# First stage of a two-layer graph network: the last removal round of each block without its ranks and its removal, with the order of the steps planned anew

## The chip, the cores and the metric

The kernel runs on one core of one Trainium2 chip, as one launch. The metric is the device time of that launch in microseconds (us); lower is better. Engine names are those of the profile: PE is TensorE (PEld its weight loads), DVE is VectorE, ACT is ScalarE, POOL is GpSimd, SP is SyncE, which here issues nearly all transfers.

## What is computed

The inputs are node features `x` (16 graphs, 1024 nodes, 128 features), a weighted adjacency `adj` (16 x 1024 x 1024, some 6% of it nonzero, diagonal set) and a node mask. Two layers follow, and the change touches only the stage that holds the first one.

```python
# layer 0
h = maximum(layernorm(x), 0)
for W, b in three layers:
    h = h @ W + b
    nh = h / maximum(norm(h), 1e-12)
    h = (adj * (nh @ nh.T)) @ h          # relu but for the last
x = x + h
# layer 1
keep = dilate(adj > 0)                   # below
h = three SAGE convolutions with batch norm on adj * keep, and a last linear map
x = x + h
```

`dilate` goes through the nodes of a graph in order. For node n it counts the neighbours that are left (num), takes sf = ceil(num/2) if num > 10 and 1 otherwise, ranks the neighbours by a running count, and removes those whose rank is a multiple of sf, from row n and from column n at once. So earlier rows change the later ones. This removal depends on `adj` alone and not on layer 0.

## The kernel before, in words

**Stages.** `build` runs four stages one behind the other: a short setup, `layer0` (the first stage of this text), `layer1_middle` and `layer1_last`. Between the first two a branch looks at one flag; if it is above zero, `dilate_all` computes the removal anew the slow way. With these inputs it is not taken.

**Two jobs in one stage.** `layer0` does layer 0 and the removal side by side.

Layer 0 is 48 *units* (16 graphs x 3 layers, lines 42 and 316 to 403), two graphs interleaved. A unit has a head and a body. The head: the product with W (`ha`, PE, L683), bias (`hb`, DVE, L869), squares with their sums (`sq`, ACT, L784), the norm (`hc`, `hd`, L873, L789, L877), the rows scaled by 1/norm (`hd`, ACT, 8 instructions at L794), 8 transposes (`hf`, PE, L639), and two copies to PSUM's outside, a rounded part (`hf`, ACT, L801) and the rest (`ho`, DVE, L881). For the first layer of a graph a layer norm comes ahead of it: statistics (`lna`, DVE, L852 and L855), 8 scaled copies (`lnb`, ACT, L767), 8 transposes (`lnc`, PE, L639). The body is 16 steps (8 blocks of 128 rows x 2 halves of 512 columns), done in pairs: two cosine tiles of three matmuls each (L702 to L704), two products with the adjacency on DVE (`cos`, L889), two aggregations (`agg`, L711, two records each). A cosine tile waits until DVE has read the tile two before it (one PSUM bank for each half). The head of unit u+1 is worked in among the body of unit u.

The removal is 32 *blocks*: 4 quads of graphs x 8 blocks of 128 rows. A block does four graphs at once. Within a block the rows depend on each other, so the kernel iterates: it guesses which entries of the diagonal 128 x 128 part go, counts, and corrects the guess, ROUNDS = [2, 3, 4, 6, 6, 3, 3, 8] times for the eight blocks of a quad, 35 rounds a quad and 140 in all. A round is
- `rank` on PE (L734, 4 matmuls into PSUM bank D0): running counts;
- `rule` on DVE (L953 to L967, 9 instructions on 4 columns): sf and the constants of each row;
- `rank` on ACT (L822, 4 instructions): the ranks of the entries, read from D0;
- `drop` on DVE (L974, 1 instruction): what remains, written to one of two tiles `Sd`.

After the last round come `bias` (DVE, L981 to L992), `check` (DVE, L1000: the last two guesses must agree, else the flag counts up) and the 8 `wide` steps, which carry the result to all 1024 columns: PE (L744, 4 matmuls into the one bank D1), ACT (L832, 2 instructions), DVE (L1006). The next block of the same quad needs the wide steps (`low` on DVE, L905 and L909) and then starts with `cross` (DVE, L921 and L925, which also reuses `check`'s scratch tile `Au`) and `base`. Rows of the adjacency come in by SP (L615) and become signs on ACT (`row`, L815), then a transpose by DMA (`fill`, L600). Finished tiles are transposed back (`flip`, L608) and multiplied (`mask`, DVE, L1018); each of these 256 mask tiles is stored by SP (L621) from a ring of three. Two quads run interleaved, first 0 and 1, then 2 and 3.

**What sets the order.** Every engine gets its instructions as one list, and the lists are made at build time by a planner (`Planner.order`, L245). Each step has a cost in ns, a rank (lower goes first) and what it comes after:

```python
def add(self, engine, name, cost, rank, after=(), chain=None, takes=None, frees=None):
...
rank = s.rank - (t - ready) / AGING
if best is None or (t, ENGINES.index(e), rank, ready) < best[:4]:
```

The planner plays the stage through with these costs and writes down the order in which the steps start; `takes` and `frees` stand for rings of buffers and the two PSUM banks. On the chip the order of each engine is fixed by this list, and only semaphores move the times. If a cost is too short in the plan, the engine that waits for the step is given it too early and stands still. SP's issue of a transfer has a cost of 70 in the plan (L242).

The steps that this text comes back to, with their plan costs: `lnb` 1610 (L339, L390), `hd` on ACT 1610 (L350), `row` 620 (L423), `check` 610 at rank 6 (L441), `mask` 620 at rank 3 (L454), `rank` on ACT 1365 (L438), `drop` 610 (L439).

## Time and profile before

| | |
|---|---|
| median of 3 runs | 2694.39 us (2693.61 to 2701.42) |
| the profiled execution | 2693.11 us, its span 2691.3 us |
| PE busy, whole span | 2579.7 us, 96% |
| DVE busy | 2076.1 us, 77% |
| ACT busy | 1459.3 us, 54% |
| first aggregation of layer 0 to its last | 34.7 to 1625.3 us |
| mean granted TensorE clock | 0.993 of full speed |

The span is the time between the first and the last instruction of the program; 1.8 us of the profiled execution lie around it. The first stage is the first 1626 us. Busy times are unions of the instructions' durations. Matmuls are pipelined, and a record's duration reaches over the start of the next.

### The profile page before, as it was taken

The numbers are of one execution on the slowest core, as the hardware profiler recorded it, in microseconds if no ns is written. First come the engines' busy times: TensorE is split into PE (matmuls) and PEld (weight loads), VectorE is DVE, ScalarE is ACT, GpSimd is POOL, SyncE is SP. The second block draws the span as 40 slices with busy tenths as digits, with TensorE's granted clock in tenths as the row PEclk, the third lists the DMA queues.
The fourth block names the chain that finished last, engine by engine and source line by source line (L and its number), as shares of the span: only waits on it lengthen the run. The fifth ranks groups of instructions, "written<-read, shape, count | busy, mean of one in ns | idle before, by whom it ended". The sixth has DMA issues, their size and how long they took to land. (4 is left out here: it accounts for less than half of the span.)

```text
span 2691.3 us, 38914 instructions
## 1 busy us (share of the span) xinstructions
PE 2579.7 (96%) x12390; PEld 1630.3 (61%) x12390; DVE 2076.1 (77%) x5328; ACT 1459.3 (54%) x4324; POOL 562.7 (21%) x233
## 2 busy tenths in 40 slices
PE   6999999999999999899999998999999999999898
PEld 4666656656655666566666654555555555555897
DVE  4778889888988888888988877766666636776676
ACT  5667747766655776567656321322322344443676
POOL 0000000000000000000000002766666603433673
PEclk9999999999999999999999999999999999999999
DMA  7354275265367244536433323555555419996663
GB/s 235 89 148 147 57 187 156 65 160 167 77 170 220 83 136 133 128 100 192 114 112 120 83 69 140 195 191 192 193 192 192 182 55 384 404 402 263 249 233 153
DMA packets 325878, 455.48 MB, mean 169 GB/s; under 512 B 155680, under 2 KB 218528, under 8 KB 325664
## 3 DMA queue, kind: packets, MB, share of 16 engines
q1 hardware_dynamic: 325664, 452.89, 51.9%
q8 instruction: 102, 1.67, 0.3%
q14 instruction: 112, 0.92, 0.1%
HBM read 352.13 MB, written 67.11 MB: 156 GB/s over the span
## 5 line engine op out<-in xcount | busy, mean ns | idle before, releaser
L711 PE MATMUL a_acc<-a_ew,a_Hr 128*128 128x512 f32 x1536 | 751.9, 600 | 0.5 <-ACT a_hT L807 0.4
L889 DVE TENSOR_TENSOR a_ew<-adj,a_cos 128x512 f32<-128x512 f32 x768 | 508.6, 682 | 68.3 <-PE a_cos L704 66.0
L1720 POOL TENSOR_TENSOR b_dsum<-adj 128x1024 f32<-128x1024 f32 x15 | 133.3, 8885 | 1797.4 <-DVE adj L1628 1797.4
L702 PE MATMUL a_cos<-a_nh 128*128 128x512 f32 x768 | 413.3, 538 | 14.0 <-DVE a_ew L889 7.3
L711 PEld LDWEIGHTS a_acc<-a_ew,a_Hr 128*128 128x128 f32 x1536 | 275.2, 190 | 160.7 <-issue 112.2
L832 ACT ACTIVATE a_v<-a_D,a_wb,a_small 128x256 f16<-128x256 f32 x512 | 287.8, 635 | 86.4 <-PE a_D L744 84.5
L704 PE MATMUL a_cos<-a_nh,a_nl 128*128 128x512 f32 x768 | 304.1, 396 | 0.0
L703 PE MATMUL a_cos<-a_nl,a_nh 128*128 128x512 f32 x768 | 301.6, 393 | 0.0
L822 ACT ACTIVATE a_vr<-a_D,a_small 128x128 f16<-128x128 f32 x560 | 209.4, 456 | 135.3 <-DVE a_small L967 134.7
L1383 PE MATMUL b_acc<-adj,b_z 128*128 128x512 f32 x512 | 225.0, 592 | 0.0
L1480 PE MATMUL b_acc<-adj,b_z 128*128 128x512 f32 x512 | 222.5, 592 | 0.0
L815 ACT ACTIVATE a_Ab<-stage 128x512 fp8e4<-128x512 f32 x256 | 156.7, 633 | 111.2 <-DMA stage<-in_adj 110.5
L1724 POOL TENSOR_TENSOR b_dsum<-b_dsum,adj 128x1024 f32<-128x1024 f32 x90 | 211.4, 2349 | 12.9
L702 PEld LDWEIGHTS a_cos<-a_nh 128*128 128x128 f32 x768 | 145.5, 189 | 101.4 <-issue 44.1
L1018 DVE TENSOR_TENSOR a_kp<-a_T,stage 128x512 fp8e4<-128x512 fp8e4 x256 | 170.0, 686 | 41.4 <-DMA scr_keep<-a_kp 39.2
L1006 DVE SCALAR_TENSOR_TENSOR a_T<-a_v,a_Ab 128x512 fp8e4<-128x512 f16 x256 | 172.2, 685 | 29.0 <-ACT a_v L832 28.6
L703 PEld LDWEIGHTS a_cos<-a_nl,a_nh 128*128 128x128 f32 x768 | 146.3, 191 | 64.2 <-issue 51.4
L1480 PEld LDWEIGHTS b_acc<-adj,b_z 128*128 128x128 f32 x512 | 96.0, 190 | 114.3 <-issue 113.1
L704 PEld LDWEIGHTS a_cos<-a_nh,a_nl 128*128 128x128 f32 x768 | 144.7, 188 | 33.4
L1383 PEld LDWEIGHTS b_acc<-adj,b_z 128*128 128x128 f32 x512 | 94.8, 190 | 107.1 <-issue 107.1
L784 ACT ACTIVATE h<-a_Hr 128x128 f32<-128x128 f32 x384 | 113.1, 299 | 69.2 <-DVE a_Hr L869 69.1
L1515 ACT ACTIVATE b_z<-b_o 128x128 f32<-128x128 f32 x256 | 75.3, 297 | 116.9 <-DVE b_o L1699 100.6
(269 smaller groups left out, 4337.6 us busy)
## 6 DMA issues: line engine op xcount, KB each, us to landing
adj<-in_adjT SPq DMA_DIRECT2D x108, 1024.0 KB, 12.8
adj<-in_adjT SPq DMA_DIRECT2D x128, 512.0 KB, 4.3
stage<-in_adj SPq DMA_DIRECT2D x256, 256.0 KB, 3.3
scr_keep<-a_kp SPq DMA_DIRECT2D x256, 64.0 KB, 1.8
scr_z<-b_zT SPq DMA_DIRECT2D x32, 512.0 KB, 3.6
scr_ag<-b_a SPq DMA_DIRECT2D x32, 512.0 KB, 3.3
stage<-scr_keep SPq DMA_DIRECT2D x13, 1024.0 KB, 7.5
b_kp<-scr_keep SPq DMA_DIRECT2D x12, 1024.0 KB, 7.8
```

Source lines behind the costliest of these rows:

```text
L702: e.matmul(cos[j][:], n[:, blk(k)], n[:, half(j)], start=True, stop=False)
L703: e.matmul(cos[j][:], n[:, blk(k)], m[:, half(j)], start=False, stop=False)
L704: e.matmul(cos[j][:], m[:, blk(k)], n[:, half(j)], start=False, stop=True).then_inc(E["cos"], 1)
L711: e.matmul(acc[j][:], Hr[u % 2][:, k, :], ew[idx % EW][:], start=(k == 0), stop=(k == NK - 1)).then_inc(E["agg"], 1)
L822: e.activation(vr[p][:, i, :], D0[:, i, :], ACT.Abs, bias=sm[p]["b2"][:, i:i + 1], scale=sm[p]["sc"][:, i:i + 1]).then_inc(T["vr"], 1)
L832: t = e.activation(v[c % 3][:, g * 256:g * 256 + 256].rearrange("p (x s) -> p s x", s=2), D1[:, 2 * g:2 * g + 2, :], ACT.Abs, bias=wb[p][: ...
L889: e.tensor_tensor(ew[idx % EW][:], adj[g % 2][:, k, half(j)], cos[j][:], ALU.mult).then_inc(E["ew"], 1)
L1006: e.scalar_tensor_tensor(TT[:, slot, 2 * j:2 * j + 2, k].rearrange("p m x s -> p m (x s)"), v[c % 3][:].rearrange("p (m c) -> p m c", m=2) ...
L1018: e.tensor_tensor(as_blocks(kp[c % 3][:]), row_half(slot, j, q), turned[:, :, :, :, q % 2], ALU.mult, saturate=False).then_inc(T["kp"], 1)
L1383: t = e.matmul(acc[j][:], src[:, q, :], adj[n % 3][:, q, half(j)], start=(q == 0), stop=(q == NK - 1))
L1480: t = e.matmul(acc[j][:], z[m % 2][:, q, :], adj[slot(m)][:, q, half(j)], start=(q == 0), stop=(q == NK - 1))
L1724: e.tensor_tensor(d, d, b[:, q, :], ALU.add).then_inc(E["ds"], 1)
```

## The change

1. In the last round of a block, `rank` on ACT (4 instructions) and `drop` on DVE (1 instruction) are gone. `rank` on PE and `rule` stay, since the wide step needs the constants; D0 is free when `rule` is done.
2. The 8 `wide` steps on PE read the guess of the round before, and so may start a round earlier. Their ACT part waits for `bias` as before.
3. `check` waits for the wide steps that contain the block's own diagonal part, computes from them and `X` what `drop` would have, with one DVE instruction more, waits for that, and compares as before.
4. Costs and ranks of the plan are other numbers, so that the lists of all engines come out anew: `lnb` 3080, `hd` 2340, `sq` at rank 0, `row` 540, `mask` 605 at rank 2, `check` 1220. The arithmetic of these steps is as before, and the layer norm's scaled copies are ACT's as before.
5. One semaphore more. The form of `frees` is another, with the same meaning for the flips.

```diff
@@ -19,7 +19,7 @@
 NK = 8
-BANK = 76
+BANK = 77
 MAGIC = 8388608.0
@@ -30,7 +30,7 @@
 MID = 1
-SQ = 1
+SQ = 0
 GAP = 0.2
@@ -291,7 +291,7 @@
             if s.frees:
-                ring, key = (s.frees, s.name) if s.frees in rings else (s.frees[0], s.frees)
+                ring, key = (s.frees, s.name) if s.frees in rings else s.frees
                 free[ring][held[(ring,) + key]] = s.end
@@ -336,7 +336,7 @@
             add("dve", ("lnb", g), 400, 1, [("act", "lna", g)])
-            add("act", ("lnb", g), 1610, 0, [("dve", "lnb", g)] + ([("pe", "hf", 0)] if g == 1 else []))
+            add("act", ("lnb", g), 3080, 0, [("dve", "lnb", g)] + ([("pe", "hf", 0)] if g == 1 else []))
             add("pe", ("lnc", g), 880, 0, [("act", "lnb", g)] + bank)
@@ -347,7 +347,7 @@
         add("dve", ("hd", v), 210, 1, [("act", "hc", v)])
-        add("act", ("hd", v), 1610, 0, [("dve", "hd", v)])
+        add("act", ("hd", v), 2340, 0, [("dve", "hd", v)])
         add("pe", ("hf", v), 880, 0, [("act", "hd", v)])
@@ -420,7 +420,7 @@
                          None, "af")
-                add("act", ("row", n, i, j), 620, 2, [("dma", "row", n, i, j)], None, None, "af")
+                add("act", ("row", n, i, j), 540, 2, [("dma", "row", n, i, j)], None, None, "af")
             transfer(("fill", n, i), 800, freed + [("act", "row", n, i, j) for j in range(2)])
@@ -434,14 +434,16 @@
             add("pe", ("rank", n, r), 260, 1, [("dve", "drop", n, r - 1)] if r else ready, None, "D0")
-            add("dve", ("rule", n, r), 1140, 3, [("pe", "rank", n, r)] + ([] if r else [("dve", "base", n)] + done))
-            add("act", ("rank", n, r), 1365, 1, [("dve", "rule", n, r)], None, None, "D0")
-            add("dve", ("drop", n, r), 610, 3, [("act", "rank", n, r)] + ([] if r else [("dve", "cross", n)]))
+            add("dve", ("rule", n, r), 1140, 3, [("pe", "rank", n, r)] + ([] if r else [("dve", "base", n)] + done), None,
+                None, ("D0", ("rank", n, r)) if r == K - 1 else None)
+            if r < K - 1:
+                add("act", ("rank", n, r), 1365, 1, [("dve", "rule", n, r)], None, None, "D0")
+                add("dve", ("drop", n, r), 610, 3, [("act", "rank", n, r)] + ([] if r else [("dve", "cross", n)]))
         add("dve", ("bias", n), 700, 3, [("dve", "rule", n, K - 1)])
-        add("dve", ("check", n), 610, 6, [("dve", "drop", n, K - 1)])
+        add("dve", ("check", n), 1220, 6, [("dve", "wide", n, i, k // 4) for i in range(Q)])
         for i in range(Q):
             for j in range(2):
-                add("pe", ("wide", n, i, j), 330, 1, [("dve", "drop", n, K - 1)], None, "D1")
+                add("pe", ("wide", n, i, j), 330, 1, [("dve", "drop", n, K - 2)], None, "D1")
                 add("act", ("wide", n, i, j), 960, 1, [("pe", "wide", n, i, j), ("dve", "bias", n)], None, "v", "D1")
@@ -450,8 +452,8 @@
                     for q in (2 * m, 2 * m + 1):
-                        last = ("flip", quad, i, m, j) if q % 2 else None
-                        add("dve", ("mask", quad, i, q, j), 620, 3, [("dma", "flip", quad, i, m, j),
+                        last = ("flip", ("flip", quad, i, m, j)) if q % 2 else None
+                        add("dve", ("mask", quad, i, q, j), 605, 2, [("dma", "flip", quad, i, m, j),
                             ("dve", "wide", quad * NK + q, i, j)], f"flip{quad}{i}{m}{j}", "kp", last)
@@ -476,7 +478,7 @@
                    "bst bag lnsd lnrs lnm lnr " + " ".join(f"adj{i}{k}" for i in range(2) for k in range(NK)))
-        T = P.sems("at0 at1 fl0 fl1 fl2 fl3 af0 af1 af2 sign low au x bs b0 b1 ct ru vr sd v8 wb wd av rw kp kps0 kps1 kps2 sum tot flag")
+        T = P.sems("at0 at1 fl0 fl1 fl2 fl3 af0 af1 af2 sign low au x bs b0 b1 ct ru vr sd again v8 wb wd av rw kp kps0 kps1 kps2 sum tot flag")
         W, rows = P.sb("W", [128, 3, 128]), P.sb("rows", [128, 3, 128])
@@ -650,6 +652,8 @@
                         e.wait_ge(T["b0"], nth["dve", "base", a[0]])
+                    elif kind == "rank" and a[1] == ROUNDS[a[0] % NK] - 1:
+                        e.wait_ge(T["ru"], 9 * nth["dve", "rule", a[0], a[1]])
                     elif kind == "rank":
@@ -737,12 +741,12 @@
                     k, K, p = n % NK, ROUNDS[n % NK], n // NK % 2
-                    e.wait_ge(T["sd"], nth["dve", "drop", n, K - 1])
+                    e.wait_ge(T["sd"], nth["dve", "drop", n, K - 2])
                     take("D1", step)
 ...
                         t = e.matmul(D1[:, b:b + 2 - odd, :],
-                                     Sd[p][K % 2][:, i, :] if q == k else at_blocks(Q * p + i, q, k),
+                                     Sd[p][(K - 1) % 2][:, i, :] if q == k else at_blocks(Q * p + i, q, k),
                                      C["UL"][:, 0:128 if odd else 256], start=(b == 0), stop=(b == 3),
@@ -992,8 +996,12 @@
                     n, = a
-                    p, c = n // NK % 2, nth["dve", "check", n]
-                    e.wait_ge(T["sd"], nth["dve", "drop", n, ROUNDS[n % NK] - 1])
+                    k, p, c = n % NK, n // NK % 2, nth["dve", "check", n]
+                    e.wait_ge(T["rw"], max(nth["dve", "wide", n, i, k // 4] for i in range(Q)))
+                    e.wait_ge(T["ct"], nth["pe", "rank", n, ROUNDS[k] - 1])
+                    e.scalar_tensor_tensor(Sd[p][ROUNDS[k] % 2][:], TT[:, slots(n), k // 2, k, :, k % 2], 0.0, X[p][:],
+                                           ALU.is_equal, ALU.is_lt, saturate=False).then_inc(T["again"], 1)
+                    e.wait_ge(T["again"], c)
                     e.wait_ge(T["x"], earlier("dve", "cross", step))
```

In the diff the hunk at line 387 is left out; it sets the same cost of `lnb` (1610 to 3080) for the last graph. A line of three dots stands for unchanged lines.

## Rows read from the trace of the kernel before

**Rows 1.** Page: span, busy time by engine, and the 40 slices.
```profile
span 2691.3 us, 38914 instructions
PE 2579.7 (96%) x12390; PEld 1630.3 (61%) x12390; DVE 2076.1 (77%) x5328; ACT 1459.3 (54%) x4324; POOL 562.7 (21%) x233
...
DVE  4778889888988888888988877766666636776676
ACT  5667747766655776567656321322322344443676
```
**Rows 2.** Windows: stretch, length, busy of PE, PEld, DVE, ACT, POOL, clock, DMA.
```profile
0.00:1626.00 1626.00, 1547.40 (x7722) 985.57 (x7722) 1366.09 (x3689) 1017.84 (x2843) 1.54 (x9) 1.00 0.47 131
1626.00:2691.30 1065.30, 1032.28 (x4668) 644.75 (x4668) 710.05 (x1639) 441.44 (x1482) 561.19 (x224) 0.99 0.61 228
...
200.00:400.00 200.00, 191.42 (x965) 121.91 (x965) 171.74 (x495) 133.93 (x374) 0.00 (x0) 0.98 0.49 129
1200.00:1400.00 200.00, 196.28 (x1023) 125.26 (x1021) 178.56 (x452) 140.53 (x383) 0.00 (x0) 1.00 0.50 142
```
**Rows 3.** Windows of single units, columns as above.
```profile
362.50:397.30 34.80, 31.64 (x147) 19.49 (x145) 29.53 (x65) 14.56 (x44) 0.00 (x0) 0.95 0.90 218
1078.60:1115.10 36.50, 31.60 (x141) 19.84 (x141) 29.34 (x48) 22.25 (x58) 0.00 (x0) 1.00 0.64 155
911.30:943.70 32.40, 32.40 (x180) 20.86 (x177) 25.00 (x58) 26.59 (x69) 0.00 (x0) 1.00 0.47 130
1510.10:1538.80 28.70, 27.70 (x106) 17.52 (x105) 24.34 (x40) 7.33 (x28) 0.00 (x0) 1.00 0.36 85
```
**Rows 4.** Waits of PE, 100 to 1500 us: total us, times, longest.
```profile
PE a_pp L639 <- ACT h L767: 13.1, 14, 1.7
PE a_D L744 <- ACT a_v L832: 11.4, 8, 3.6
PE a_pp L639 <- ACT h L794: 7.9, 11, 3.2
PE a_cos L702 <- DVE a_ew L889: 6.0, 7, 1.3
PE a_cos L702 <- DVE a_nl L881: 3.3, 7, 1.0
```
**Rows 5.** Waits of DVE, 100 to 1500 us.
```profile
DVE a_ew L889 <- PE a_cos L704: 40.7, 58, 1.5
DVE a_kp L1018 <- DMA scr_keep<-a_kp: 27.8, 31, 2.4
DVE a_T L1006 <- ACT a_v L832: 25.7, 34, 3.4
DVE a_Sd L974 <- ACT a_vr L822: 25.0, 33, 2.0
```
**Rows 6.** Groups by line in the first stage: busy, mean ns of one.
```profile
L832 ACT ACTIVATE a_v<-a_D,a_wb,a_small 128x256 f16<-128x256 f32 x512 | 287.8, 635 | 86.4 <-PE a_D L744 84.5 <-DVE a_T L1006 1.8
L822 ACT ACTIVATE a_vr<-a_D,a_small 128x128 f16<-128x128 f32 x560 | 209.4, 456 | 135.3 <-DVE a_small L967 134.7
L1018 DVE TENSOR_TENSOR a_kp<-a_T,stage 128x512 fp8e4<-128x512 fp8e4 x256 | 170.0, 686 | 41.4 <-DMA scr_keep<-a_kp 39.2
L974 DVE SCALAR_TENSOR_TENSOR a_Sd<-a_vr,a_X 128x512 fp8e4<-128x512 f16 x140 | 96.1, 686 | 27.0 <-ACT a_vr L822 26.8
L925 DVE SCALAR_TENSOR_TENSOR a_X<-a_T,a_Au 128x512 fp8e4<-128x512 fp8e4 x32 | 22.1, 692 | 1.1
L1000 DVE SCALAR_TENSOR_TENSOR a_Au<-a_Sd 128x512 fp8e4<-128x512 fp8e4 x32 | 22.0, 687 | 0.4
```
**Rows 7.** Timeline of ACT, end of block 3: start, us.
```profile
309.37 2.45 ACT L794 ACTIVATE h<-a_Hr,a_rnrn 128x128 f32<-128x128 f32 x8 [0.77 <-DVE a_rnrn L877]
311.73 1.48 ACT L822 ACTIVATE a_vr<-a_D,a_small 128x128 f16<-128x128 f32 x4
313.10 1.01 ACT L801 ACTIVATE a_nh<-a_pp 128x1024 fp32r<-128x1024 f32 x1
```
**Rows 8.** Line L767, eight scaled copies of a layer norm: ns min/median/max.
```profile
L767 ACT ACTIVATE h<-h,a_lnnm,a_lnrs x120: 477/479/497, 8.7 to 1458.4; 128x128 f32<-128x128 f32 x120
```
**Rows 9.** Timeline of DVE, three places.
```profile
53.49 0.69 DVE L921 SCALAR_TENSOR_TENSOR a_Au<-a_Ab,tri 128x512 fp8e4<-128x512 fp8e4 x1 [0.91 <-DMA a_T<-a_Ab]
54.22 0.69 DVE L925 SCALAR_TENSOR_TENSOR a_X<-a_T,a_Au 128x512 fp8e4<-128x512 fp8e4 x1
54.83 0.68 DVE L889 TENSOR_TENSOR a_ew<-adj,a_cos 128x512 f32<-128x512 f32 x1
...
312.46 0.18 DVE L992 TENSOR_TENSOR a_wb<-a_wb,a_small 128x16 f32<-128x16 f32 x1
313.24 0.69 DVE L974 SCALAR_TENSOR_TENSOR a_Sd<-a_vr,a_X 128x512 fp8e4<-128x512 f16 x1 [0.59 <-ACT a_vr L822]
313.96 0.69 DVE L1000 SCALAR_TENSOR_TENSOR a_Au<-a_Sd 128x512 fp8e4<-128x512 fp8e4 x1
...
1089.23 0.68 DVE L889 TENSOR_TENSOR a_ew<-adj,a_cos 128x512 f32<-128x512 f32 x1
1093.36 0.69 DVE L1006 SCALAR_TENSOR_TENSOR a_T<-a_v,a_Ab 128x512 fp8e4<-128x512 f16 x1 [3.45 <-ACT a_v L832]
```
**Rows 10.** Timeline of ACT at the longest stall of PE.
```profile
1085.39 1.12 ACT L832 ACTIVATE a_v<-a_D,a_wb,a_small 128x256 f16<-128x256 f32 x2 [0.34 <-PE a_D L744]
1091.69 0.63 ACT L815 ACTIVATE a_Ab<-stage 128x512 fp8e4<-128x512 f32 x1 [5.17 <-DMA stage<-in_adj]
1092.23 1.10 ACT L832 ACTIVATE a_v<-a_D,a_wb,a_small 128x256 f16<-128x256 f32 x2
```
**Rows 11.** Masks on DVE and aggregations on PE: first and last start.
```profile
L1018 DVE TENSOR_TENSOR a_kp<-a_T,stage x256: 641/685/695, 329.3 to 1583.9; 128x512 fp8e4<-128x512 fp8e4 x128
...
L711 PE MATMUL a_acc<-a_ew,a_Hr x1536: 590/592/1061, 34.7 to 1625.3; 128*128 128x512 f32 x192
```

More of the change, by code:

```diff
@@ L389, in plan_units @@
     add("dve", ("lnb", G), 400, 1, [("act", "lna", G)])
-    add("act", ("lnb", G), 1610, 1, [("dve", "lnb", G), ("pe", "hf", 3 * G - 1)])
+    add("act", ("lnb", G), 3080, 1, [("dve", "lnb", G), ("pe", "hf", 3 * G - 1)])
     add("act", ("first", 0), 920, 3, [("act", "lnb", G)])
```

## The prediction

> **What bounds the kernel now.** I read the page first. The program has 38914 instructions in 2691.3 us; PE is busy 96% of it, DVE 77%, ACT 54% [rows 1]. The DVE slices stand at 8 and 9 from the fourth to the 21st and are lower behind it: the removal loads DVE in the first stage. The windows then split the span: the first stage is 1626 us with 1547 us of PE, 1366 of DVE and 1018 of ACT; the other 1065 us hold nothing that the change touches, so they stay as they are [rows 2]. In the middle of the stage both engines are nearly full at once: from 200 to 400 us PE 191 and DVE 172 of 200, from 1200 to 1400 us PE 196 and DVE 179 [rows 2]. The clock stood at 0.98 to 1.00 of full speed there, its upper level of 2.4 GHz.
>
> Then I cut out single units of layer 0. A unit in which the removal makes no rounds any more takes 28.7 us. One with rounds but no masks takes 32.4 us; two with rounds and masks take 34.8 and 36.5 us, though PE had 31.6 us of busy time in both [rows 3]. So the stage's time is the sum of PE's own work and of short stalls, and the stalls are worst where removal rounds, masks and bodies share DVE. The removal itself sets no end: its last mask starts at 1583.9 us and the last aggregation at 1625.3 [rows 11]. An earlier end of the removal is thus worth nothing by itself. What counts is how long PE stands.
>
> Where it stands, by PE's waits from 100 to 1500 us: 13.1 us before the transposes of a layer norm (14 times, so 0.94 each), 7.9 before those of a head (11 times, 0.72 each), 11.4 for ACT to empty D1 (8 times), 6.0 for DVE's product and 3.3 for its last copy of a head [rows 4]. That is some 42 us that can be seen. Waits of DVE in the same stretch: 27.8 for stores of masks, 25.7 and 25.0 for ACT's parts of wide step and round [rows 5].
>
> **The change, part by part.**
>
> *The last round's ranks on ACT.* 560 instructions for 140 rounds are 4 each and 209.4 us, 1.50 us a round [rows 6]. One round in each of 32 blocks goes: 32 x 1.50 = 48 us off ACT's 1018. ACT is at 63% of the stage and not the bound, so this comes through only where PE waits for ACT. In the timeline a last round's ranks (1.48 us at 311.73) stand between the end of the scaling of a head (309.37 + 2.45) and the copy at 313.10 that the head still needs [rows 7]. Of the 11.4 us for D1 the longest, 3.6, has another cause: ACT sat 5.17 us before a row of the adjacency came in, with the wide step behind it in its queue [rows 10]. I give this part 2 us, between 0 and 8 (11.4 less 3.6).
>
> *The last `drop` and the new test.* One instruction of 686 ns goes, 32 times. One of the same kind comes in `check`: 128 x 512 elements, read strided out of `a_T`, as `cross` does in 692 ns [rows 6]. So 0 us of DVE work, where I had looked for a saving. What does go is DVE's wait for ACT in that round: 25.0 us in 140 rounds, 32/140 of it 5.7 us, and at the last round of block 3 it was 0.59 us [rows 5, 9]. What comes is a wait of DVE for itself, between the test and the comparison. `cross` has the same pair: its second starts 0.73 us after the first, the next free instruction 0.61 after that one [rows 9]. So 0.12 us x 32 = 4 us more of DVE. Net 2 us of DVE given back, of which PE sees perhaps all: 2 us, between -4 and +6. The Trainium skill (VectorE: DVE Perf Modes, "The DRAIN you can't avoid") says that a semaphore between two Vector instructions costs nothing extra, since the next one waits for the pipe in any case. By it the 4 us would be 0 and the gain of this part 6; the rows speak against it, so the sum goes by them.
>
> *The wide steps' PE part a round earlier.* The same 8 x 4 matmuls. They hide beside `rank` and `rule`, but the first holds D1 until `bias` is done, and `base` of the other quad also needs D1. The trace has no such hold to read. The nearest rows bound it from both sides: if one wide step in a block finds D1 taken, or is spared a wait, that is at most one of the 11.4/8 = 1.4 us waits, and with some of 32 blocks hit either way a few us. I take 0, as the plan knows D1's ring, between -3 and +3.
>
> *`check` behind the wide steps, `cross` behind `check`.* `check` is last in rank, and the next block's `cross` needs its scratch tile. So between a block's wide steps and the next block's first `drop` stand two more instructions of 0.69 and a read-out. Against this each block's chain loses 1.50 of ACT and 0.69 of DVE and their signals, 2.2 us or more. The chain gets shorter on balance, and it has no end to set [rows 11]: 0.
>
> *New costs in the plan.* This is the largest term. Eight instructions of `lnb` at 479 ns with some 0.09 of overlap are about 3.2 us, where the old plan had 1.61; eight of `hd` took 2.45 us against 1.61 [rows 7, 8]. The old plan thus handed PE the transposes 1.5 and 0.7 us (3.08 less 1.61, 2.34 less 1.61) too early, and the stalls before them, 0.94 and 0.72 each, are of that size [rows 4]. With 3.08 and 2.34 PE is given a pair of cosine tiles or an aggregation in that time instead, and the head still has most of a 32 us unit to finish. Of 13.1 + 7.9 = 21.0 us, two thirds should go: 14 us, between 5 and 21. `row` at 540 and `check` at 1220 are small repairs. `mask` goes to rank 2, ahead of `rule` and `drop`; that is the part I trust least (below).
>
> *A new order as such.* Each unit's stalls depend on what happens to stand beside what: single units range from 28.7 to 36.5 us [rows 3]. The two with rounds and masks differ by 1.7 us; with 48 units and about 1.5 us of such scatter in each, the sum scatters by the root of 48 times that, about 10 us. I take 0 for it and keep 10 either way for the range.
>
> *Sum.* 2 + 2 + 0 + 0 + 14 = 18 us. The profiled execution took 2693.1 us (2691.3 of span and 1.8 around it), so it would take 2675; the median of the runs is 1.3 above the profiled one, which gives 2676.5.
>
> **The rivals.**
>
> *DVE is the bound, nothing comes of it (22%).* In the middle of the stage DVE was busy 172 to 179 us of 200, its work does not shrink, and and PE's stalls before cosine tiles would just grow by what those before transposes lose. Against it: in units without masks DVE had 7.4 of 32.4 us to spare [rows 3]. The Trainium skill speaks for it (Trainium Kernel Development and Optimization, "Performance Expectations"): matmul busy time is a bad measure of nearness to the limit, weight loads are the good one, and for other engines occupancy is fine. In rows: weight loads 61% in the stage, DVE 84% [rows 2]. In that case only the 2 us of DVE come out: 2692.
>
> *Masks crowd DVE (10%, slower).* At rank 2 the masks of a flip go ahead of rules and drops, in runs. They are stored from a ring of three, so the fourth in a run waits for a store, and while DVE stands there no product is made and PE stands before its next cosine tile. DVE lost 39.2 us to this in the stage [rows 6], and a unit with masks cost 2.4 to 4.1 us more than one without [rows 3]. If that wait doubled and PE saw it all, it would be +39 against the -18: 2715. It decides from about 18 us more, from which on the kernel is no faster; above 26 it is slower. For it: of SP's transfers each store stands in one queue with the rows and transposes, and these aren't repriced. Against it: 256 masks are the same number, a plan that knows the ring spreads them, and a unit of 28.7 us late in the stage, while masks still run, shows that masks alone do no harm [rows 3, 11].
>
> *Larger than forecast (8%).* If the stalls of crowded units shrink too, because rounds of 140 are 108 for ACT, and half of the 42 seen and half of the 27.8 for stores go, it is 35 us: 2659; with the hidden part of stalls, which lie inside long matmul records, 2650.
>
> *The change does not do what it says (under 1%).* The round on PE and `rule` stay, and only ACT's instructions go; that is visible in the counts and no doubt about time. I leave it in the rest.
>
> **How the numbers follow.** The forecast's case has 60%, 2660 to 2690. The range takes in the bounds of the terms: at best 8 + 6 + 3 + 21 = 38 us, so 2656, rounded to 2655; at worst the DVE rival with scatter, 2702. Beyond lie most of the masks' case and the lowest end of the larger one. A difference of 0.3%, 8 us, is about what a measurement of this kernel can tell from no change: faster means under 2686.3, slower over 2702.5. Faster: four fifths of the 60 and all of the 8, and a sixth of the rival of DVE by scatter, 0.63 in all rounded up to 0.65; slower 0.11; the same 0.24.
>
> **What would show it.** Right: L822 x432 for 560 and L974 x108 for 140, beside `check`'s two instructions of 32 each; ACT's busy time down by 48 us, DVE's within 5; PE's waits before L639 down to a third of 21 us; the second stage 1065 us as before; last aggregation near 1607; the last mask before 1584. Wrong: the waits before L639 gone and those of L702 or the mean of L702 (a stall hides in its record) grown by as much, which is the DVE rival; the DVE wait for stores well above 39 us, which is the masks'; or waits before L639 as they were, which would say that the plan's costs were not their cause.

## The result, and the profile after

The changed kernel took 2705.11 us (median of 6 runs, 2703.74 to 2706.85) against 2694.72 for the kernel before on the same chip; the ratio is 1.0033, with a 95% interval of 1.0022 to 1.0043. It is slower, by 10 us in the medians and 9 by the ratio, where I had forecast 18 us less. The profiled execution has a span of 2702.0 us.

The page of the changed kernel, its first lines:

```profile
span 2702.0 us, 38818 instructions
PE 2582.3 (96%) x12390; PEld 1642.4 (61%) x12390; DVE 2079.9 (77%) x5328; ACT 1418.1 (52%) x4196; POOL 562.3 (21%) x233
```

128 instructions of ACT are gone and its busy time fell by 41 us [rows 1], where I had put 48. DVE has the same count and 4 us more. Windows of the changed kernel, columns as in [rows 2], the stage now ending at 1636 us:

```profile
0.00:1636.00 1636.00, 1547.98 (x7722) 995.80 (x7722) 1370.01 (x3689) 977.41 (x2714) 1.55 (x9) 0.99 0.47 130
1636.00:2702.00 1066.00, 1034.29 (x4669) 646.64 (x4668) 709.92 (x1639) 440.71 (x1482) 560.74 (x224) 0.98 0.61 228
```

The second part is as long as before (1066 against 1065 us); the whole difference lies in the first stage, where PE has the same 7722 instructions and as much busy time, in 10 us more. Groups of the first stage by line, which answer to [rows 6]:

```profile
L836 ACT ACTIVATE a_v<-a_D,a_wb,a_small 128x256 f16<-128x256 f32 x512 | 287.2, 631 | 116.4 <-PE a_D L748 71.9 <-issue 31.2 <-DVE a_wb L996 10.1
L1026 DVE TENSOR_TENSOR a_kp<-a_T,stage 128x512 fp8e4<-128x512 fp8e4 x256 | 170.5, 686 | 49.0 <-DMA scr_keep<-a_kp 46.3
L826 ACT ACTIVATE a_vr<-a_D,a_small 128x128 f16<-128x128 f32 x432 | 161.8, 455 | 126.7 <-DVE a_small L971 126.7
L978 DVE SCALAR_TENSOR_TENSOR a_Sd<-a_vr,a_X 128x512 fp8e4<-128x512 f16 x108 | 73.9, 685 | 17.3 <-ACT a_vr L826 17.0
L1008 DVE SCALAR_TENSOR_TENSOR a_Au<-a_Sd 128x512 fp8e4<-128x512 fp8e4 x32 | 22.1, 692 | 1.1
L1002 DVE SCALAR_TENSOR_TENSOR a_Sd<-a_T,a_X 128x512 fp8e4<-128x512 fp8e4 x32 | 22.0, 688 | 0.3
```

The ranks on ACT fell from 209.4 to 161.8 us, the 48 us of the forecast for this group; one `drop` of 686 ns went for one test instruction of 688. ACT waits 10.1 us for `bias` (`a_wb`) at wide steps whose PE part came early. Now PE's waits from 100 to 1500 us, which answer to [rows 4], and DVE's, which answer to [rows 5]:

```profile
PE a_D L748 <- ACT a_v L836: 21.3, 18, 4.4
PE a_cos L706 <- DVE a_nl L885: 14.9, 9, 4.7
PE a_cos L706 <- DVE a_ew L893: 7.6, 8, 1.6
PE a_D L738 <- DVE a_Sd L978: 5.2, 6, 2.0
PE a_pp L641 <- ACT h L798: 2.5, 1, 2.5
```

```profile
DVE a_kp L1026 <- DMA scr_keep<-a_kp: 36.2, 37, 2.7
DVE a_T L1014 <- ACT a_v L836: 26.7, 37, 2.3
DVE a_Sd L978 <- ACT a_vr L826: 16.2, 26, 2.2
```

The waits before transposes went from 13.1 + 7.9 to 2.5 us, nearly all of them. But PE's wait for ACT to empty D1 rose from 11.4 to 21.3, for the last copy of a head (`a_nl`) from 3.3 to 14.9, for the product from 6.0 to 7.6, and 5.2 for `Sd` were under 1. These four rose by some 27 us where those before transposes fell by 18.5: the stalls changed places and grew by some 9 us, about the loss. The whole stage says the same. From 100 us to the last aggregation PE was busy 1471.6 us of 1525.3 before and 1472.5 of 1535.4 after; the gaps between its records grew from 53.7 to 62.9 us.

The stalls are also fewer and longer. Of gaps over 1.3 us there were 6 before (14.9 us together) and 19 after (43.2 us). That shows in the clock. Before, the granted clock of the stage fell to 0.50, the lower level of 1.2 GHz, three times, 10.2 us in all; after, eight times, 34.0 us. Each time it fell during a stall of PE or within 2 us of its end, the shortest of these stalls being 1.26 us long. Here are two of the stretches after, then a stall of PE in its timeline and the stretch that follows it; columns of the windows as in [rows 2]:

```profile
378.70:385.50 6.80, 5.11 (x39) 3.27 (x40) 5.14 (x9) 3.17 (x10) 0.00 (x0) 0.50 0.88 251
747.40:754.20 6.80, 5.13 (x11) 2.62 (x11) 4.36 (x8) 5.79 (x24) 0.00 (x0) 0.50 0.67 169
...
882.73 0.50 PE L706 MATMUL a_cos<-a_nh 128*128 128x512 f32 x1 [3.69 <-DVE a_nl L885]
...
883.90:887.30 3.40, 3.40 (x8) 1.66 (x6) 3.40 (x6) 0.60 (x1) 0.00 (x0) 0.50 0.36 96
```

Half the clock for 24 us more is worth up to 12 us of PE's work, by my estimate. It doesn't explain the loss by itself: e1, e3 and e14 below are 8 to 12 us slower than the kernel before with only 10, 17 and 20 us at the lower level. How much of the changed kernel's loss it makes is not shown.

The removal also ends later. Last wide steps and last masks of the changed kernel:

```profile
L1014 DVE SCALAR_TENSOR_TENSOR a_T<-a_v,a_Ab x256: 639/684/694, 64.0 to 1561.8; 128x512 fp8e4<-128x512 f16 x128
...
L1026 DVE TENSOR_TENSOR a_kp<-a_T,stage x256: 639/685/695, 335.5 to 1608.7; 128x512 fp8e4<-128x512 fp8e4 x128
```

The last mask starts 25 us later than before [rows 11] although each block has a shorter chain.

### The profile page after: what moved, and what is told of

Read it like the earlier page. It is cut to its first block and busy times, and to the rows that moved or that the text cites. A ratio compares the mean times of both kernels' runs of the same rounds, so it can differ in the third digit from the quotient of the medians.

```text
span 2702.0 us, 38818 instructions
## 1 busy us (share of the span) xinstructions
PE 2582.3 (96%) x12390; PEld 1642.4 (61%) x12390; DVE 2079.9 (77%) x5328; ACT 1418.1 (52%) x4196; POOL 562.3 (21%) x233
## 5 line engine op out<-in xcount | busy, mean ns | idle before, releaser
L715 PE MATMUL a_acc<-a_ew,a_Hr 128*128 128x512 f32 x1536 | 761.4, 605 | 2.2 <-DVE a_ew L893 1.8
L706 PE MATMUL a_cos<-a_nh 128*128 128x512 f32 x768 | 425.1, 553 | 27.6 <-DVE a_nl L885 17.2
L826 ACT ACTIVATE a_vr<-a_D,a_small 128x128 f16<-128x128 f32 x432 | 161.8, 455 | 126.7 <-DVE a_small L971 126.7
L706 PEld LDWEIGHTS a_cos<-a_nh 128*128 128x128 f32 x768 | 146.8, 191 | 120.2 <-issue 45.7
L1026 DVE TENSOR_TENSOR a_kp<-a_T,stage 128x512 fp8e4<-128x512 fp8e4 x256 | 170.5, 686 | 49.0 <-DMA scr_keep<-a_kp 46.3
L748 PE MATMUL a_D<-UL,a_T 128*128 128x128 bf16 (+1 forms) x896 | 122.1, 247 | 19.6 <-ACT a_v L836 19.5
```

The costliest lines, as they stand in the source:

```text
L706: e.matmul(cos[j][:], n[:, blk(k)], n[:, half(j)], start=True, stop=False)
L715: e.matmul(acc[j][:], Hr[u % 2][:, k, :], ew[idx % EW][:], start=(k == 0), stop=(k == NK - 1)).then_inc(E["agg"], 1)
L826: e.activation(vr[p][:, i, :], D0[:, i, :], ACT.Abs, bias=sm[p]["b2"][:, i:i + 1], scale=sm[p]["sc"][:, i:i + 1]).then_inc(T["vr"], 1)
L1026: e.tensor_tensor(as_blocks(kp[c % 3][:]), row_half(slot, j, q), turned[:, :, :, :, q % 2], ALU.mult, saturate=False).then_inc(T["kp"], 1)
```

## The experiments

The changed arithmetic and the changed order came together, so the runs take them apart. `before` is the kernel before on the same chip, 2694.8 to 2697.6 us. Ratios are given to it, with 95% intervals. Differences in us are of medians unless it says otherwise; by the ratios the larger ones come out 1 to 3 us smaller.

### The new arithmetic in the old order

**e1_frozen.** The lists are those of the plan before, with steps struck and moved afterwards:

```diff
+    out["act"] = [s for s in out["act"] if not (s[0] == "rank" and last(s))]
+    dve = [s for s in out["dve"] if not (s[0] == "drop" and last(s)) and s[0] != "check"]
+    for s in [s for s in out["dve"] if s[0] == "check"]:
+        n = s[1]
+        need = [("wide", n, i, n % NK // 4) for i in range(Q)]
+        at = max(dve.index(w) for w in need) + 1
+        dve.insert(at, s)
```

> The arithmetic of the changed kernel (last rank and drop of a block gone, test behind the wide steps) in the order of the kernel before: the last ranks of ACT and the last drops of DVE are struck from its lists, each check is moved to just behind the wide steps it reads, the final tally behind that, and nothing else is planned anew. Theory O (the loss is the new order's, the removed round is worth a little): 2 to 12 us below the kernel before, some 2686 to 2692, waits of PE before L706's counterpart for the last copy of a head near the 3.3 us of before. Rival S (the new structure costs: the test, D1 held by the early wide steps): 3 us or more above the kernel before.

2706.7 us, ratio 1.0038 (1.0023 to 1.0052). My theory falls and rival S stands: in this order the new structure is 10 us slower. Which part of it, three more runs tell.

**e8_frozen_nocheck** is e1 with the 32 checks struck too, and with them the wait of `cross` and of the final tally for a check (the last guess is tested by nothing). Against e1:

```diff
-        dve.insert(at, s)
+        at = at
```

> The kernel with the order of before and the last rounds struck out, now without the 32 checks and their comparisons (the flag stays at zero, nothing tests the last guess). Theory T (the late test is what the order of before has no room for on DVE): it takes back most of the 10 us by which the frozen order with checks was over the kernel before, 2690 to 2698. Rival D (the cost of the frozen order is the wide steps' hold on D1 or the struck waits, not the test): 2702 or more.

2689.3 us, 0.998 (0.997 to 0.9989), the fastest of all. **e9_before_nocheck** strikes the checks from the kernel before (again nothing tests the guess):

```diff
+    out["dve"] = [s for s in out["dve"] if s[0] != "check"]
```

> The kernel before in its own order with the 32 checks struck out (0.77 us of DVE each, at the place right behind the last drop); nothing tests the last guess. Theory T (what costs is DVE time in places where DVE is full; behind the last drop DVE waits anyhow, so the check there is nearly free): 2689 to 2695, less than 6 us gained. Rival W (DVE work costs the same wherever it stands, some 0.3 us for each us as between the two frozen orders): 2686 to 2688. Either way the difference to 2689.3 of the frozen order without checks is what striking 32 ranks and drops is worth by itself.

2696.7 us, 1.0006 (0.9996 to 1.0016): the check behind the last drop cost nothing where it stood. **e10_late_single** keeps all rounds and moves the one comparison behind the wide steps:

```diff
+        dve.insert(max(dve.index(("wide", n, i, n % NK // 4)) for i in range(Q)) + 1, s)
```

> The kernel before in its own order and with all its rounds; only each check, still one comparison, is moved from behind the last drop to behind the wide steps that the changed kernel waits for, and the final tally behind that. Theory T (the place costs): 3 to 10 us slower than before, 2698 to 2705. Rival W (it is the second instruction of the test, not the place): within 2 us of before.

2699.7 us, 1.0019 (1.0009 to 1.0028), 3 us over the kernel without checks. The last aggregation of these four (line of PE, first and last start). First e9:

```profile
L716 PE MATMUL a_acc<-a_ew,a_Hr x1536: 590/592/1168, 35.4 to 1625.9; 128*128 128x512 f32 x192
```

Then e10, its comparison late:

```profile
L724 PE MATMUL a_acc<-a_ew,a_Hr x1536: 590/592/1163, 35.2 to 1631.7; 128*128 128x512 f32 x192
```

e8, the last rounds struck and no checks:

```profile
L732 PE MATMUL a_acc<-a_ew,a_Hr x1536: 590/592/1168, 35.0 to 1620.5; 128*128 128x512 f32 x192
```

and e1, the same with the late test:

```profile
L732 PE MATMUL a_acc<-a_ew,a_Hr x1536: 590/592/1057, 35.1 to 1634.8; 128*128 128x512 f32 x192
```

So with the order held, striking the last ranks and drops is worth 2689.3 - 2696.7 = -7.4 us by medians (5.4 in the profiles). By the intervals of the two ratios this is 7 us, give or take 4. One comparison in the late place costs 3.0 us (5.8) over the kernel without any, for 0.77 x 32 = 25 us of DVE work; the test's two instructions cost 17.4 us (14.3) for 1.46 x 32 = 47 us. DVE work that is free while DVE waits for ACT costs, set behind the wide steps without a plan, between 0.12 and 0.37 of its length (3.0/25 and 17.4/47); the 3.0 is no larger than the interval of the two ratios, so the lower end is loose. In e1 this is how the pair stands, in the timeline of DVE:

```profile
84.33 0.69 DVE L1031 SCALAR_TENSOR_TENSOR a_T<-a_v,a_Ab 128x512 fp8e4<-128x512 f16 x1 [1.28 <-ACT a_v L853]
85.06 0.69 DVE L1019 SCALAR_TENSOR_TENSOR a_Sd<-a_T,a_X 128x512 fp8e4<-128x512 fp8e4 x1
85.78 0.69 DVE L1025 SCALAR_TENSOR_TENSOR a_Au<-a_Sd 128x512 fp8e4<-128x512 fp8e4 x1
86.40 0.08 DVE L1025 DVE_READ_ACCUMULATOR a_Au<-a_Sd 128x1 f32 x1
86.40 0.68 DVE L910 TENSOR_TENSOR a_ew<-adj,a_cos 128x512 f32<-128x512 f32 x1
```

The product of a cosine tile stands behind the pair, and PE's cosine matmul behind that product. The starts of 0.72 to 0.73 us apart are the self-wait that I had put at 0.12 us each. There are two of them where I had counted one: the test waits for the wide step just ahead of it, and the comparison for the test.

**e16_split_test** sets the two instructions apart: the first stays, the second goes just ahead of the next block's `cross`.

```diff
+        dve.insert(at, ("again", n))
+        place = dve.index(("cross", after[0])) if after else at + 9
+        dve.insert(place, s)
```

> The frozen order without the last rounds, with the test's two instructions apart: the first behind the wide steps, the second just ahead of the next block's cross, other work of DVE between them, so that DVE doesn't wait for itself. Theory T (the late test costs by DVE's time in full places, and by its own wait): back by 3 to 10 us from the 2706.7 of the frozen order, 2696 to 2703. Rival (it is the amount of DVE work alone): 2704 or more.

2708.5 us, 1.0041 (1.0027 to 1.0055), no better than e1. The wait between the two isn't what costs. That it is the amount of work, in either late place, fits this run and is not shown beyond it.

**e12_pool_check** gives the test to POOL, which is idle in this stage, with multiplications, additions and subtractions on `X` and `Sd` in place:

```diff
+                e.tensor_tensor(X[p][:], TT[:, slots(n), k // 2, k, :, k % 2], X[p][:], ALU.add, saturate=False).then_inc(T["v8"], 1)
...
+                e.tensor_tensor(X[p][:], X[p][:], guess[:], ALU.subtract, saturate=False).then_inc(T["v8"], 1)
...
+                e.tensor_tensor(guess[:], X[p][:], X[p][:], ALU.mult, saturate=False).then_inc(T["v8"], 1)
...
```

> The order of before with the last rounds struck out and the test done by POOL, which has nothing to do in this stage: five instructions of 128 x 512 and four of 128 x 128 a block on POOL, none on DVE. Theory T: near the frozen order without checks, 2688 to 2694, and below both kernels. Rival K (POOL and DVE share a way to the memory, or the next block's cross waits for POOL): 2698 or more, with products on DVE longer than 682 ns or waits of DVE for POOL.

2734.4 us, 1.0145 (1.0128 to 1.0162), 45 us over e8, which has the same lists and no test. Rival K stands. One of POOL's groups and three of DVE's, first stage of e12, then the masks' durations (ns, min/median/max):

```profile
L874 POOL TENSOR_TENSOR a_X<-a_X,a_Sd 128x512 fp8e4<-128x512 fp8e4 x32 | 41.0, 1281 | 2.5
...
L937 DVE TENSOR_TENSOR a_ew<-adj,a_cos 128x512 f32<-128x512 f32 x760 | 503.8, 682 | 69.9 <-PE a_cos L726 67.1
L1059 DVE SCALAR_TENSOR_TENSOR a_T<-a_v,a_Ab 128x512 fp8e4<-128x512 f16 x256 | 186.7, 742 | 28.7 <-ACT a_v L854 28.2
L1071 DVE TENSOR_TENSOR a_kp<-a_T,stage 128x512 fp8e4<-128x512 fp8e4 x256 | 185.0, 746 | 33.3 <-DMA scr_keep<-a_kp 31.2
...
L1071 DVE TENSOR_TENSOR a_kp<-a_T,stage x256: 640/686/1614, 336.2 to 1623.0; 128x512 fp8e4<-128x512 fp8e4 x128
```

The two groups of DVE with both inputs in SBUF grew from some 686 to 742 and 746 ns on average, some 30 us over both. But their median stayed at 686: of the 256 masks the 35 that ran while POOL did took 1126 ns on average, up to 1614, and the other 221 took 686. The product, which reads one input from PSUM, stayed at 682, and at 678 in the 118 that ran beside POOL. DVE also waited 7.9 us for POOL once, before the final tally (L978).

### The new order

**e11_after_nocheck** is the changed kernel, new order and all, with its checks struck from DVE's list by the line of e9 (nothing tests the guess).

> The changed kernel in its own new order with the 32 checks of two instructions struck out; nothing tests the last guess. If the late test costs in the new order what it cost in the order of before (17 us between the two frozen orders), 2686 to 2693. Rival (the new order has room for it, since it was planned with it at 1220): 2699 or more.

2707.7 us, 1.0039 (1.0025 to 1.0053): not faster than the changed kernel. In the new order, planned with it, the test costs nothing that shows. But the same arithmetic without a test takes 2689.3 us in the old order and 2707.7 in the new one. **For this arithmetic the new order costs 18 us** (16 by the ratios).

That is one of two ways to split the loss. Without the test: -7 for the struck work (e9 to e8), +18 for the order (to e11), -3 for the test put back. With the test in the old order: -7, then +17 for the test (e1), then -2 for the new order. Both end at the changed kernel, 8 us over e9. The new lists were made with 1220 ns for each test in them, and no run plans the arithmetic without a test for itself; so the parts hold only along their way.

The plan's numbers one by one, each on the kernel before or taken back in the changed kernel:

**e2_costs_only**: `before` with all of them, rounds and check unchanged. The lines are shown in part; the same change of `lnb` for the last graph is left out.

```diff
-SQ = 1
+SQ = 0
-            add("act", ("lnb", g), 1610, 0,
+            add("act", ("lnb", g), 3080, 0,
-        add("act", ("hd", v), 1610, 0,
+        add("act", ("hd", v), 2340, 0,
-                add("act", ("row", n, i, j), 620, 2,
+                add("act", ("row", n, i, j), 540, 2,
-                        add("dve", ("mask", quad, i, q, j), 620, 3,
+                        add("dve", ("mask", quad, i, q, j), 605, 2,
```

The next ones take single pairs of these lines, forward or back, and add `-FIRST = 10`, `+FIRST = 12`.

> The kernel before with only the new plan numbers (lnb 3080, hd 2340, sq rank 0, row 540, mask 605 at rank 2), rounds and check as before. Theory H (with the true costs of a head the transposes come later, the stalls before them go and come back as waits for the head's last copy at a unit's start): waits of PE before transposes under 5 us, waits for a_nl 10 us or more, time 2695 to 2708. Rival O1 (the repaired costs help by themselves, the loss is from planning the shorter block): 2675 to 2688. Rival M (masks at rank 2): waits of DVE for stores over 42 us in the stage.

2726.6 us, 1.0115 (1.0093 to 1.0136), the slowest of the new orders and beyond what I expected. The waits of PE went as theory H has it: none to speak of before transposes, 11.7 for `a_nl` and 24.5 for D1.

**e13_heads_only**: `before` with 1610 to 3080 and 1610 to 2340 alone.

> The kernel before with only the true costs of the heads in the plan (lnb 3080, hd 2340). Theory H (most of the 31 us by which all new numbers together made the kernel before slower comes from these two): waits before transposes gone, time 2710 to 2725, waits of PE for ACT to empty D1 and for a_nl up. Rival M (the mask's rank): 2690 to 2702.

2707.1 us, 1.0034 (1.0023 to 1.0045), less than the 2710 that I expected at least. Its PE waits, 100 to 1500 us:

```profile
PE a_D L744 <- ACT a_v L832: 15.0, 13, 2.7
PE a_cos L702 <- DVE a_nl L881: 11.4, 6, 2.8
PE a_D L734 <- DVE a_Sd L974: 10.0, 9, 2.8
PE a_pp L639 <- ACT h L794: 5.5, 3, 3.3
...
PE a_pp L639 <- ACT h L767: 2.5, 4, 1.0
```

Here nothing but two costs of the plan changed. The waits before transposes fell from 21.0 to 8.0 us; those for D1, `a_nl` and `Sd` rose from some 15 to 36.4. This is the trade of the changed kernel by itself, at a loss of 12 us (9 by the ratio). The clock stood at the lower level for 37.5 us here.

**e14_mask_only**: `before` with `mask` at 605 and rank 2 alone.

> The kernel before with only mask at cost 605 and rank 2. Theory M: 5 to 12 us slower than before, as going back on it made the changed kernel 7 us faster, 2700 to 2707. Rival (no effect of its own, the 7 us were another order's luck): 2690 to 2699.

2707.3 us, 1.0035 (1.0022 to 1.0049), 12 us slower, with DVE's waits for stores at 38.1 us in the stage, where the kernel before has 39.2. **e4_mask_old**: the changed kernel with `mask` back at 620 and rank 3.

> The changed kernel with mask back at cost 620 and rank 3. Theory M (masks ahead of rules and drops crowd DVE): waits of DVE for stores back to 39 us or less and 5 to 12 us faster than the changed kernel, 2693 to 2700. Theory H: the waits for a_nl stay and the time stays within 5 us of 2705.

2698.1 us, 1.0004 (0.9994 to 1.0014), 7 us better than the changed kernel. But its waits for stores did not fall to 39 us (45.0 in the stage). In neither run do they follow the time, so they aren't how the rank costs.

**e15_heads_old**: the changed kernel with the heads back at 1610.

> The changed kernel with lnb and hd back at 1610 in the plan. Theory H: 8 us or more faster than the changed kernel, under 2697, with waits before transposes of some 20 us back. Rival L (a new order gives what it gives; the two terms aren't additive): 2698 to 2715.

2703.7 us, 1.0023 (1.0014 to 1.0033), 1 to 3 us better, with 22.7 us of waits before transposes back: 12 us in one kernel, 2 in the other. Theory H had asked for 8 or more. **e3_struct_only**: the changed kernel with all the old numbers.

> The changed kernel with the old plan numbers for lnb, hd, sq, row and mask; only the block is shorter and check costs 1220 behind the wide steps, planned anew. Theory H: waits before transposes are back near 20 us, those for a_nl near 3, time 2685 to 2696. Rival S: 2700 or more. Theory L (any new order scatters by some 10 us): no tie between time and the numbers changed.

2704.6 us, 1.0026 (1.0014 to 1.0037). Waits before transposes were back (21.4 us), time was not; theory H had 2696 at most. Then numbers that mean little: **e7_sq0** (`before`, `SQ = 0`), **e18_row_only** (`before`, `row` at 540), **e17_after_sq1** (changed kernel, `SQ = 1`).

> The kernel before with only the rank of the squares at 0: everything planned anew from a change that means next to nothing, with the quads in step as before. It shows how far a new order as such moves the time. Theory L (orders scatter): anything from 2684 to 2708. Theory P with little scatter: 2691 to 2699.

2697.5 us, 1.0009 (1.0 to 1.0019).

> The kernel before with only row at 540 in the plan, the smallest of the changed numbers. Theory L together with the finding that each of the new orders tried so far was slower than the order of before: 2696 to 2708. Rival (a more truthful plan is better or equal): 2688 to 2696.

2709.5 us, 1.0049 (1.0033 to 1.0066): 80 ns of cost in the plan, 12 to 13 us on the chip.

> The changed kernel with only the rank of the squares back at 1, which means next to nothing by itself and plans everything anew. Theory L (orders scatter by 5 to 10 us from a small number anywhere): a time off the changed kernel's 2705 by 4 us or more, either way, within 2692 to 2718. Rival (the changed kernel's loss is fixed by its arithmetic and costs): within 3 us of 2705.

2713.7 us, 1.0053 (1.0037 to 1.0069), 9 us above the changed kernel.

Two runs tested a mechanism. In the changed kernel the last quad's blocks trail their partner's by 60 to 130 us. **e5_in_step** binds them in the plan alone (lines shown in part):

```diff
+        mate = [("dve", "wide", n + NK - 1, i, j) for i in range(Q) for j in range(2)] if k and not p else []
-        ready = gate + (filled
+        ready = gate + mate + (filled
```

> The changed kernel with one more dependence in the plan alone, none on the chip: a block of the leading quad starts after the wide steps of the partner quad's block before it, so that the two quads of a pair stay within about a block of each other (in the trace of the changed kernel the blocks of quads 2 and 3 are 60 to 130 us apart from block 26 on, before the change 10 to 40 us). Theory P (the loss comes from the two quads drifting apart in the new order, which leaves the last quad's rounds alone at the end and late): the last wide step back from 1562 to some 1510 to 1530 us, time 2692 to 2700. Rival N (drift is harmless, the new order loses by its many small waits): 2702 to 2710.

2707.9 us, 1.0047 (1.003 to 1.0064). The last wide step came 22 us earlier (1539.5), not as early as expected, the last mask 24 us later (1632.6), and the time did not fall. So this run did only half of what it should. e17 settles more: its removal ends even before that of the kernel before (last mask 1577.3 against 1583.9 us), and it took 2713.7 us. A late end of the removal is not the cause. **e6_apart** (`before`, `FIRST = 12`) has the quads apart with all else equal:

> The kernel before with FIRST 12 instead of 10, its arithmetic, costs and ranks untouched: in this order the two quads run 40 to 170 us apart almost from the beginning. Theory P: 2704 to 2725, last mask 20 us later or more. Rival N, drift is harmless: 2690 to 2700.

2713.9 us, 1.0069 (1.0052 to 1.0086). That agrees with P, and just as well with any new order, as e18 shows.

| order | ratio to before |
|---|---|
| arithmetic of before, six new orders (e7, e13, e14, e18, e6, e2) | 1.0009, 1.0034, 1.0035, 1.0049, 1.0069, 1.0115; mean 1.0052 |
| changed arithmetic with its test, six new orders (e4, e15, e3, changed kernel, e5, e17) | 1.0004, 1.0023, 1.0026, 1.0033, 1.0047, 1.0053; mean 1.0031 |

All twelve new orders are at or above the time of the kernel before, two of them (e4, e7) within its noise. They aren't twelve independent draws, since several share the heads' costs or the masks' rank. Over orders the changed arithmetic is the better one, by 0.0021 or 6 us in the means, near the 7.4 us that the frozen order gave for the struck work; the scatter within a row is as large, so the means alone would not show it. The order of the kernel before is an uncommonly good one, and each change tried gives it up. Why it is good I haven't shown.

What the slow ones have in common can be read from the traces. From 100 us to the last aggregation, length and gaps of PE are 1520.5 and 48.9 us in e8, 1525.3 and 53.7 in `before`, 1534.8 and 61.5 in e1, 1535.4 and 62.9 in the changed kernel, 1539.1 and 64.1 in e13, 1547.9 and 70.6 in e17, 1558.0 and 75.0 in e2. Most of each loss is time in which PE stands, whatever the stall is for.

## Why the prediction was wrong

- **The last round's ranks and drop** (forecast: 48 us off ACT, 0 us of DVE work). The ranks' work was right to the microsecond (ACT's busy time as a whole fell by 41). Its worth fits as well: 7.4 us in a held order, where my two terms without the test's self-wait, 2 for PE's waits and 5.7 for DVE's, make 7.7. With an interval of 4 us either way, that they agree so closely is luck.
- **The test behind the wide steps** (forecast: 4 us of DVE for the self-wait, nothing else). Half wrong. The sum counted DVE's work by amount, and took out and put in the same 0.69 us. The old place was free (e9), the new one is not: 17 us in the old order without a plan for it (e1 against e8). Where the plan knows of it, it cost nothing measurable (e11). So taking it out does not give back the changed kernel's loss; what an order planned without it would take is open.
- **New costs in the plan** (forecast: -14 us). This is the step that failed. The mechanism that I read was real: the stalls before transposes came from too short costs, and they went, 21.0 to 2.5 us. But I booked their end as a gain. PE stood instead for the head's last copy at unit starts (3.3 to 14.9 us) and for D1 at wide steps (11.4 to 21.3), in fewer and longer stalls. e13, with nothing else changed, cost 12 us; in the changed kernel taking the two costs back gave 1 to 3 (e15). So the term was +1 to +12 by the kernel it stands in, and in neither -14. That what was put ahead of the transposes pushed the other steps back fits these waits; it is argued from the lists, not shown.
- **A new order as such** (forecast: 0, 10 us either way). The size was right, the centre was not. Six new orders of unchanged arithmetic lie from +2 to +31 us, 14 in the mean. The bound that I should have written is one-sided: an order can be as good as this one, and none of twelve was better.
- **`check` on the chain, D1 held early** (forecast: 0 each). The removal ended later, not earlier, and e17 says that the late end is not what costs. ACT's 10 us for `bias` show that D1 was held, but in the old order the early wide steps added only 1 us to PE's waits for D1 (13.9 in e9, 14.8 in e8), and e13, without them, has 15.0.
- **Rivals.** That DVE is the bound and nothing comes of it: its sign came true for the most part. Where 18.5 us before transposes went, PE's waits at L706 are 13 us above those of L702 before (9.7 to 22.5), and the mean of that matmul rose from 536 to 553 ns, partly by the lower clock. But without 47 us of DVE work the changed kernel was no faster (e11), so the amount of DVE work is not what bounds it. Masks at rank 2, the slower rival: taking the rank back gave 7 us and setting it alone cost 12, so the number matters as it gives another order; its mechanism, the waits for stores, grew by 7 us where I had supposed 39 (39.2 to 46.3), and in e4 they stayed while the time fell.
- **The Trainium skill.** Its page VectorE: DVE Perf Modes, "The DRAIN you can't avoid", has the semaphore between two Vector instructions at no extra cost. The test and its comparison start 0.72 us apart in e1, with no wait for another engine, the comparison and the next product 0.62. So the trace disagrees by 0.1 us each time; but with the two set apart (e16) nothing was gained. Whether the time was nearer to the rule's 0 or to my 4 us the runs can't tell, as their intervals are of that size.
- **The chances.** Four fifths of 60, all of 8 and a sixth of 22 are 0.60, not the 0.63 that I wrote for "faster"; and the DVE slices stand at 8 and 9 up to the 23rd, not the 21st. Neither touches the forecast.

Open stays which property of the old order makes it good, what part the lower clock behind long stalls has in the loss, why the heads' costs are worth 12 us in one kernel and 2 in the other, and how much of the 17 us for the unplanned test lies at which block.

## What to carry to other kernels

In a kernel whose engines follow lists written by a planner, a removed piece of work and the new order must be measured apart: strike the step from the old lists first, and only then plan anew. A stall that a truer cost will remove is not a gain until the trace shows what PE waits for instead; count all waits of the engine, not those of the line. Look at the length of stalls as well as their sum, since here the clock fell at long ones. And a new order can lose by the scatter of orders alone (here 2 to 31 us in 2695 with the arithmetic unchanged), so take several before judging the change.

## What the hardware showed that I had not expected

POOL's tensor operations on 128 x 512 fp8 elements took 1.2 to 1.28 us each. While they ran, DVE's instructions with both inputs in SBUF took up to 1.6 us for 0.69: 35 of 256 masks met them, with 1126 ns on average, and the other 221 stayed at 686. The mean of 746 ns looks like 8% for everyone and is a long wait for a few. The product, with one input in PSUM, was at 678 ns beside POOL and 682 else. An engine that is idle is not free: 266 us of work on POOL went with a time 45 us above e8.

In the first stage the granted clock fell to the lower level three times before and eight times after, for 3.4 or 6.8 us each, and each time in a stall of PE or just behind one, the shortest of them 1.26 us long. Not every long stall brought a fall (8 falls for 19 stalls over 1.3 us after). So a few long stalls may cost more than many short ones of the same sum; how much, these runs don't part from the stalls themselves.
